# A decoder layer's attention stage on one core: calls in a new order, and a second norm from a row sum and centred squares

## The reference

```python
# attention over head dimensions within a token, 32 heads, 8 groups, D = 32
q, k, v = [einsum('bse,edh->bsdh', x, W) + b for W, b in (q, k, v)]
k, v = repeat(k, 4, axis=-1), repeat(v, 4, axis=-1)
attn = softmax(einsum('bsdh,bseh->bsde', q, k) / sqrt(D), axis=-1)
x1 = layernorm(x + einsum('bsde,bseh->bsdh', attn, v).reshape(...))
# cross product with the context, both quantised to 0..255 and back
x2 = layernorm(x1 + matmul(fake_quant(x1), fake_quant(ctx)))
# feed forward: relu(x2 up)^2 down + gated (x2 fc1 expert) fc2
out = layernorm(x2 + ffn(x2))          # ffn ends in its own norm
def layernorm(x, eps=1e-5): return (x - mean(x)) / sqrt(var(x) + eps)
```

## Time and profile before

| | us |
|---|---|
| median of 3 runs | 703.67 |
| lowest, highest | 699.07, 710.43 |
| the profiled execution, its own time | 700.77 |
| its span, first to last instruction | 698.6 |
| busy: TensorE, weight loads | 613.8, 492.4 |
| busy: VectorE, ScalarE, GpSimd | 418.4, 292.5, 148.9 |
| mean granted clock of TensorE | 0.973 |

### The profile page before, as it was taken

How to read it: one execution, slowest core, us unless ns; L and a number is a source line. 1 busy time by engine, 2 the same in 40 slices (tenths; PEclk the granted TensorE clock), 3 DMA queues, 4 the chain that set the end, 5 groups by cost and what they waited for, 6 DMA issues and landing times.

```text
span 698.6 us, 7888 instructions
## 1 busy us (share of the span) xinstructions
PE 613.8 (88%) x2952; PEld 492.4 (70%) x2960; DVE 418.4 (60%) x552; ACT 292.5 (42%) x378; POOL 148.9 (21%) x172
## 2 busy tenths in 40 slices
PE   3698698986569889989989999999899999999992
PEld 2487476764347548858868888888688888888881
DVE  6947788998888523332443244123886456667866
ACT  4555566555463524233233253311344433422635
POOL 3424385554721311322320000000000000002100
PEclk9999999999988999999999999999999999999996
DMA  9664425442762458695888876630232223459912
GB/s 331 234 180 146 146 79 179 137 110 76 260 181 54 156 190 301 227 335 172 316 306 300 288 253 214 177 121 1 90 121 91 91 92 105 166 192 308 267 77 120
DMA packets 86326, 125.61 MB, mean 180 GB/s; under 512 B 23952, under 2 KB 54928, under 8 KB 86288
## 3 DMA queue, kind: packets, MB, share of 16 engines
q1 hardware_dynamic: 78816, 97.31, 42.3%
q0 software_dynamic: 5168, 19.40, 8.6%
q10 hardware_dynamic: 2304, 8.39, 3.5%
HBM read 85.23 MB, written 35.65 MB: 173 GB/s over the span
## 4 chain that ended last, share of the span: by engine, by line
PE 58%; DVE 19%; DMA 8%; ACT 4%; issue 4%; SPq 3%; POOL 3%; POOLq 0%; DVEq 0%; ACTq 0%
PE acc_b L1192 26%; PE acc_a L1224 14%; PE acc_b L1224 12%; DMA u_raw<-in_L_ffn_up_w_dram 2%; POOL u_raw L843 1%; SPq L243 1%; DMA x_scratch<-res 1%; DVE c_sb L709 1%; DVE stat L571 1%; PE qkv_ps L283 1%; DMA f2b<-x_scratch 1%; PE sc_ps L300 1%; ACT y_sb L425 1%; DVE u_raw L598 1%; PE xa_ps L325 1%
## 5 line engine op out<-in xcount | busy, mean ns | idle before, releaser
L1414 DVE TENSOR_TENSOR u_lo<-u_raw,u_hi 128x1024 fp32r<-128x1024 f32 x18 | 23.0, 1276 | 112.5 <-ACT u_hi L1267 112.5
L1192 PE MATMUL acc_b<-x2T_hi,u_hi 128*128 128x512 f32 x160 | 63.3, 396 | 2.7 <-DVE u_lo L1414 2.7
L1192 PE MATMUL acc_b<-x2T_hi,u_lo 128*128 128x512 f32 x160 | 62.4, 390 | 0.0
L1192 PE MATMUL acc_b<-x1T_hi,u_hi 128*128 128x512 f32 x160 | 62.3, 390 | 0.0
L1192 PE MATMUL acc_b<-x2T_lo,u_hi 128*128 128x512 f32 x160 | 62.3, 389 | 0.0
L1192 PE MATMUL acc_b<-x1T_hi,u_lo 128*128 128x512 f32 x160 | 62.3, 389 | 0.0
L1192 PE MATMUL acc_b<-x1T_lo,u_hi 128*128 128x512 f32 x160 | 62.2, 389 | 0.0
L1685 POOL DMA_DIRECT2D x1T_hi<-r_scratch x4 | 2.9, 712 | 269.4 <-PE acc_a L1224 261.4
L283 PE MATMUL qkv_ps<-w_hi,xT_hi 128*128 128x512 f32 (+1 forms) x128 | 36.1, 364 | 14.3 <-DVE w_lo L642 10.5
L1267 ACT ACTIVATE u_hi<-u_raw 128x1024 fp32r<-128x1024 f32 x18 | 19.0, 1056 | 55.1 <-DMA u_raw<-in_L_ffn_up_w_dram 32.3
L1224 PE MATMUL acc_a<-x1T_hi,x2T_hi 128*128 128x512 f32 x168 | 39.1, 389 | 0.0
(11 more groups left out here) (250 smaller groups left out, 1420.3 us busy)
## 6 DMA issues: line engine op xcount, KB each, us to landing
d_raw<-in_L_ffn_down_w_dram SPq DMA_DIRECT2D x20, 512.0 KB, 6.4
t_scratch<-d_raw SPq DMA_DIRECT2D x20, 512.0 KB, 4.5
d_raw<-t_scratch SPq DMA_DIRECT2D x20, 512.0 KB, 3.8
c_sb<-in_ctx_dram ACTq DMA_DIRECT2D x16, 512.0 KB, 4.6
u_raw<-in_L_ffn_up_w_dram SPq DMA_DIRECT2D x16, 512.0 KB, 7.3
r_scratch<-f1b SPq DMA_DIRECT2D x10, 512.0 KB, 4.1
r_scratch<-f2b SPq DMA_DIRECT2D x10, 512.0 KB, 3.1
x_sb<-in_x_dram SPq DMA_DIRECT2D x8, 512.0 KB, 4.8
```

The source lines that it names most:

```text
L1192: mm = pe.matmul(acc_b[:, q % 4], s, v, start=(k == 0 and i == 0), stop=(k == KT - 1 and i == 2))
L1414: dve.tensor_tensor(u_lo[:, m % 2], u_raw[:, m % 2], u_hi[:, m % 2].bitcast(F32), ALU.subtract).then_inc(S["u_lo_done"], 1)
```

## The change

**Order.** The loop over steps is gone. Each engine's list of calls is written out, one call a line, in an order by urgency that differs from engine to engine. Projections are split in two halves, so that another call can stand between them; loads, stores and context tiles are single calls.

**Waits and buffers.** Column sums become a call of their own, `column_sums(b)`, ahead of the batch's first quantised transpose. The values product of tiles 0 to 6 writes into `tr_ps`, the bank of the input transposes, instead of `sc_ps`: it waits for `xT_lo_done` of the transposes already placed there, and `transpose_x(t)` for t of 3 and more waits until the values of tile t - 3 are collected (`o_done`). Scores in turn wait only for the subtraction of the tile before (`sub_done`). `s_max` and `s_sum` have one slot instead of two, the norms' small buffers one per tile.

**Second norm.** VectorE adds the cross product with an instruction that also sums the rows, and scales the sum to the negated mean. ScalarE squares `res` with that mean as bias and sums the squares. GpSimd forms (squares / 1024 + eps) to the power -1/2 and, for tiles 0 to 5, the product of the negated mean with it; ScalarE then scales those tiles (`ACT_TILES`), VectorE tiles 6 and 7. The first norm is as it was.

```diff
+        ACT_TILES = (0, 1, 2, 3, 4, 5)
+        PARTS = 2
...
-        av_ps = sc_ps[:].rearrange("p (n t) d -> p n t d", n=NG)
+        av_early, av_last = tr_ps[:].rearrange("p n (t d) -> p n t d", t=TQ), sc_ps[:].rearrange("p (n t) d -> p n t d", n=NG)
+        av_of = lambda t: av_last if t == TILES - 1 else av_early
...
             def transpose_x(t):
                 pe.wait_ge(x_in[t % 2], 16 * (t // 2 + 1))
                 if t >= 1:
                     pe.wait_ge(S["xT_lo_done"], t)
+                if t >= 3:
+                    pe.wait_ge(S["o_done"], t - 2)
...
             def scores(t):
                 pe.wait_ge(S["q_bd_done"], t + 1)
                 pe.wait_ge(S["k_bd_done"], t + 1)
                 if t >= 1:
-                    pe.wait_ge(S["o_done"], t)
+                    pe.wait_ge(S["sub_done"], t)
...
             def values(t):
                 pe.wait_ge(S["smT_done"], t + 1)
                 pe.wait_ge(S["v_bd_done"], t + 1)
-                pe.wait_ge(S["sub_done"], t + 1)
+                if t < TILES - 1:
+                    pe.wait_ge(S["xT_lo_done"], min(t + 3, TILES))
+                    if t >= 1:
+                        pe.wait_ge(S["o_done"], t)
+                else:
+                    pe.wait_ge(S["sub_done"], TILES)
...
+            def column_sums(b):
+                pe.wait_ge(S["c_done"], (b + 1) * CK)
+                if b:
+                    pe.wait_ge(S["xa_evac"], b * BT)
...
+            def x2_squares(t):
+                act.wait_ge(S["nmean_done"], t + 1)
+                act.activation(xa_out[:], res[:, t % XR], ACT.Square, bias=nmean[:, t:t + 1],
+                               accum_out=squares[:, t:t + 1]).then_inc(S["st2_done"], 1)
+
+            def normalise_x2(t):
+                act.wait_ge(S["nbias_done"], ACT_TILES.index(t) + 1)
+                act.activation(res[:, t % XR], res[:, t % XR], ACT.Identity, bias=nbias[:, t:t + 1],
+                               scale=rstd[:, TILES + t:TILES + t + 1]).then_inc(S["x2_done"], 1)
...
             def cross_residual(t):
...
                 dve.wait_ge(S["x1col_done"], t + 1)
-                dve.tensor_tensor(res[:, t % XR], res[:, t % XR], xa_out[:], ALU.add).then_inc(S["x2pre_done"], 1)
...
+                dve.scalar_tensor_tensor(out=res[:, t % XR], in0=xa_out[:], scalar=1.0, in1=res[:, t % XR],
+                                         op0=ALU.mult, op1=ALU.add, accum_out=total[:, t:t + 1]).then_inc(S["x2pre_done"], 1)
                 dve.wait_ge(S["x2pre_done"], t + 1)
-                stats(t, False, S["st2_done"], S["mv2_done"])
+                dve.tensor_scalar(nmean[:, t:t + 1], total[:, t:t + 1], -1.0 / EMB, None, ALU.mult).then_inc(S["nmean_done"], 1)
...
+            def inverse_deviation_x2(t):
+                i = TILES + t
+                pool.wait_ge(S["st2_done"], t + 1)
+                pool.tensor_scalar(veps[:, i:i + 1], squares[:, t:t + 1], 1.0 / EMB, EPS, ALU.mult, ALU.add).then_inc(S["ve2_done"], 1)
+                pool.wait_ge(S["ve2_done"], t + 1)
+                pool.tensor_tensor(rstd[:, i:i + 1], veps[:, i:i + 1], so["neg_half"][:], ALU.pow).then_inc(S["rstd2_done"], 1)
+                if t in ACT_TILES:
+                    pool.wait_ge(S["rstd2_done"], t + 1)
+                    pool.tensor_tensor(nbias[:, t:t + 1], nmean[:, t:t + 1], rstd[:, i:i + 1], ALU.mult).then_inc(S["nbias_done"], 1)
```

950 lines of the change are left out of this document (622 added, 328 removed).

## The result

The changed kernel takes 672.90 us, the median of four executions (671.75 to 677.61), against 707.05 for four of the kernel before: a ratio of 0.961, with a 95% interval from 0.951 to 0.970. The profiled execution took 673.77 us, with a span of 672.0. The forecast was 672, on 700.77 for the profiled execution of before. The profiled pair fell by 27.0 us and the medians by 34.2; the profiled execution of before was one of its faster ones, with a mean clock of 0.973, where those beside the experiments have 0.948 to 0.968. The stretches of the sum went less evenly than the total, so first the table of stretches that answers to the earlier trace rows. It is cut where the projections of tiles 4 to 7 end, and its columns are again the stretch, its length, busy time of TensorE, its weight loads, VectorE, ScalarE and GpSimd, granted clock, DMA share and GB/s.

The account below looks back on a forecast made before the run. Stage one's 250 us were taken as bound by latency early, VectorE in the middle, waits in the tail. Start -7.7, three tiles -2.6 and tail -18.7 gave -29.0 on 700.77: 672 us, range 660 to 692.

Parts of the forecast that it names:

- The bound of before: Stage one: VectorE with short hand-overs bounds the middle tiles; in the last 91.9 us waits do, no engine.
- The norm, as VectorE's work: Second norm: VectorE saves 2.14 us a tile, 19.57 becoming 17.4; ScalarE's and GpSimd's added work stays hidden.
- up to 2.14 a tile: Upper bound on the norm edit's worth, in us, if VectorE sets the period.
- The start: From 30 us to projection 4's end: end moves from 98.5 to 90.8, so -7.7 us; bounds 88 to 95.
- The three tiles: Projection 4's end to projection 7's: 19.0 us a tile, 57 against 59.6, so -2.6; bounds -6.2 and +4.6.
- the 2.070 row: VectorE's fc2 remainder took 2.070 against 1.236; possible GpSimd contention, 0.83 more on 22 steps, 18 us at worst.
- 20 or 21: Period in us of a middle tile if GpSimd contention adds 2.3 a tile to VectorE at worst.
- The tail: Projection 7's end to stage two's first matmul: 73.2 us against 91.9, so -18.7; bounds 67 to 82.
- The reason given for the tail: Scores 7 stood behind tile 3's x2 store and transposed load in TensorE's order; now they precede every x2 transpose.
- The first: Rival: the order moves waits instead of removing them, period 21.4, tail 82, -13 us, 688; chance 0.19.
- The second, the bank: Rival: input transposes wait for VectorE's collect in every tile, margin 0.4 us, up to +48, 720; chance 0.04.
- The fourth: Rival: x2's round trip still ends last in stage one wherever TensorE waits for it, within 2% of 703; chance 0.07.

Follow-up runs that it names:

- e2: Kernel before with its old order, given the new second norm (row sum with the add, squares and scaling on ScalarE): 704.75 us, ratio 0.996.
- e1: Changed kernel with the new order but the old second norm, statistics and scaling on VectorE: 687.02 us, ratio 0.971.
- e7: Changed kernel with input transpose 3 and its two evacuations moved ahead of values 0: 676.33 us, ratio 0.957.
- e9: Changed kernel with GpSimd's column-term add held back in tiles 0, 2 and 6 until VectorE's first normalise of the next tile: 671.25 us, ratio 0.955.
- e5: Kernel before with scores 7 and the steps that follow from them put ahead of the first two x2 transpose groups: 707.98 us, ratio 1.001.
- e12: Kernel before with scores 7 ahead of the x2 transposes and values 6 in the bank of the input transposes: 707.26 us, ratio 0.998.
- e3: Changed kernel with the values product back in the scores' bank for all tiles: three executions at 687.4 to 689.3 us, one at 675.38, no ratio.
- e0: The changed kernel run again without any edit: 673.83 us, ratio 0.953.

## Why the prediction was right, step by step

**The bound of before** (VectorE with hand-overs in the middle, waits in the tail) stands. That in the tail no engine is the bound but waits are is what e2 shows: 11.4 us less of VectorE's work left it as long as it was.

**The norm, as VectorE's work.** The count held by kinds: eight pairs of statistics, eight aggregates and six scalings are gone, and accumulator and negated mean cost 0.08 and 0.15 a tile, as taken. The sum shows less of it, 170.3 us of VectorE's work from 30 to 250 before and 158.5 in the new stage one, since 8.4 of the former and some 15 of the latter are steps that stood behind GpSimd. The squares cost 1.147 + 0.188, as taken. What failed is the sentence on its value, that "if TensorE sets the period, the norm's edit alone is worth nothing beyond the margin it makes". It is worth 13.2 us in the new order (e1), and little of it in the period: most of it shows in the tail, which has five of the eight norms and where waits and a lower clock add to their work. How much each adds was not separated. The bound "up to 2.14 a tile", 17 over eight tiles, would have held it.

**The start** was -5.2 instead of -7.7. The term that was too small is projection 3 and values 1 at 8.32 + 1.95: they took 13.2, part of it at half clock behind 2.4 us of waiting, twice. I had counted the tail's clock as a risk and not this one. e7 shows that the hole cannot be moved away on TensorE alone. The bounds of 88 to 95 for the end of projection 4 held: 93.3.

**The three tiles** took 55.3 instead of 57: 17.0 to 17.3 of TensorE, where the sum had 17.6, and 1.7, 0.5 and 1.6 around it where it had 1.4. The larger two hold the normalises that met GpSimd: without these (e9) the period is 17.1 to 17.5, with TensorE busy for 50.9 of the 51.9 us and VectorE for 51.0, so that which of them bounds it cannot be told. The prediction saw the 2.070 row and priced such a meeting at 0.83 on 22 steps, 18 us at worst, then took none of it. The 0.83 was misread: it is the mean over one step that stood for 1.7 and one that met nothing. The kind was wrong too, since it looked at two-input steps alone and seven of the nine have one input; the product, 15, was near that worst case. It cost the period less than "20 or 21", because VectorE's own work was only 15.5 where 17.4 had been taken (17.10 in the tile of 17.5, less the 1.58 of one meeting). The 19.57 from which the 17.4 was worked out already held a meeting, 1.5 us of it.

The Trainium skill, SBUF — State Buffer, section SBUF: two separate sides, has the port pair that VectorE and GpSimd share as a lock held for a whole instruction, with the loser fully blocked. The trace agrees: 2.67 against 0.88 with an end 0.55 behind GpSimd's, and at most 0.88 again in e9 once the two are apart. The prediction cited a softer wording of it from another page; the stronger one would have priced a meeting by GpSimd's own 2.36 and 2.77 us.

**The tail** was 74.2 against 73.2, by errors that cancelled. TensorE's work was 61.1 (a few records may be missing) and not 63.8; the wait in front of the first x2 transpose 2.1 and not 6, for the collect in one trace and for the DMA in the other; the small gaps 7.9 and not 1.5, most of them in front of the quantised transposes and cross products of late tiles; the hand-over 2.8 and not 1.9, which was ScalarE's figure; the clock 0.99, as taken.

**The reason given for the tail** did not bear out, while its number was right. "The scores need none of that; they stand behind it in TensorE's order" is true of the list, but taking the scores from behind it is worth nothing (e5: 0.6 slower, not told apart from zero), nor with a bank of their own (e12: -0.1, though that edit also put two more remainders ahead of tile 7's sum). The chain of waits named the release that came last; a second one, the collect, ended within a microsecond or two of it, and VectorE's list held a third. What removes the 20.4 is in the order of the lists together, as far as the runs go: VectorE takes the maximum and sum of tile 7 ahead of the x2 remainders, SyncE stores x2 early, the weight products stand between the last tile's steps. Which of these carries most was not separated.

**The number.** That 672 was met so closely is in part luck. -29.0 was forecast; the profiled pair gave -27.0, with errors that cancelled within the tail and between the stretches; the medians gave -34.2. The forecast counted from an execution 6 us below the median of before.

**The rivals.** The first (waits moved, period 21.4) is out by the table. The second, the bank, did not come to pass: apart from transpose 3, where it was expected, the input transposes wait 0.19 to 0.42 us for the collect in front of projections 5 to 7, so the cover was as thin as said (0.4 us), and it nearly held. Whether the other choice of bank would have cost time e3 leaves open. The fourth, the round trip as the end of stage one, is out: where its wait shows at all (e0) it is 2.2 us.

## What to carry to other kernels

A wait that the chain names can hide another of the same length on another engine: before pricing its removal, read on the timeline when the next thing that the freed step needs is ready, and when the engine behind it will come to its result. Where an engine is full over many tiles, work taken from it may hardly shorten the period (1.3 us over three tiles here) and still be worth much more at the end of the stage, so judge it there. When one list is changed to test a wait, look whether the edit puts something new in the same tile's way on another engine, as e12's did. And compare the shortest and the longest duration of one operation on VectorE: where they differ by most of the length of a two-input step of GpSimd, look on both timelines whether the two meet; an added wait on GpSimd can part them, and a mean over both prices neither.

## What the runs showed of the hardware that was not expected

- A VectorE step of one SBUF input (0.63 to 0.88 us) that starts inside GpSimd's step of two SBUF inputs (2.36 or 2.77) does not end until about 0.55 after it; one of two SBUF inputs (1.16 to 1.23) not until about 1.1 after it. VectorE's steps that read a PSUM bank kept their time beside GpSimd's: the subtraction at 118.49 and the remainder of x at 119.63, beside the add from 118.09 to 120.45, took 1.22 and 1.21.
- Waits of 1.95 to 2.26 us of TensorE were followed by a granted clock of 0.83 over the next ten microseconds (e3's trace; one of its four executions kept its clock), one of 3.4 by 0.50 over four (e7), so that in such a place a wait costs nearly twice what the list of waits shows. Not every wait does: behind the 2.12 in the tail of the changed kernel the clock stayed at 1.00.
- The order and the norm together are worth some 10 us more than the sum of each alone: 20.4 and 2.7 against 33.6, where the 2.7 has an interval from 0 to 6.
